# The residual add, the FP4 rewrite and retention's two decay products move off the vector engine: a two-layer macaron block on one Trainium2 core

## The reference, cut to what matters

```
def fp4_quant_dequant(x):                       # blocks of 16 along the last axis
    scale = max(max|xb| / 6, 1e-12)
    return GRID[searchsorted(MID, |xb/scale|)] * sign(xb/scale) * scale
def fp4_linear(x, w): return fp4_quant_dequant(x) @ fp4_quant_dequant(w).T
def _L1_ffn_ref(x, w_gate, w_up, w_down):
    h = silu(fp4_linear(x, w_gate)) * fp4_linear(x, w_up)      # 352 wide
    return fp4_linear(h, w_down)
def _L1_attn_ref(x, ...):                       # retention, 16 heads of 8
    scores = (Q @ K^T) * Dm / sqrt(8)           # Dm: gamma_h ** (l - m), causal
    out = scores @ V; group norm over (8 features, all tokens); @ Wout
x = x + 0.5 * _L1_ffn_ref(_layernorm(x), ...)
x = x + _L1_attn_ref(_layernorm(x), ...)
x = x + 0.5 * _L1_ffn_ref(_layernorm(x), ...)
```

## Time and profile before

| | |
|---|---|
| median of 3 runs | 1813.59 us (1809.85 to 1815.0) |
| the profiled execution, its own time | 1820.12 us |
| its span, first to last instruction | 1818.2 us |
| busy share of the span | PE 91%, DVE 77%, ACT 54%, POOL 19% |
| FP4 layer, n = 3 | about 1399 to 1535 us of the span |
| retention | about 1528 to 1688 us |
| FP4 layer, n = 5 | about 1688 to 1818 us |

### The profile page before, as it was taken

How to read it: one execution, slowest core, us unless ns; L and a number is a source line. 1 busy time by engine, 2 the same in 40 slices (tenths; PEclk the granted TensorE clock), 3 DMA queues, 4 the chain that set the end, 5 groups by cost and what they waited for, 6 DMA issues and landing times.

```text
span 1818.2 us, 30155 instructions
## 1 busy us (share of the span) xinstructions
PE 1652.5 (91%) x10801; PEld 962.2 (53%) x10801; DVE 1406.3 (77%) x2337; ACT 990.2 (54%) x1958; POOL 345.9 (19%) x661
## 2 busy tenths in 40 slices
PE   6899999879999999999999889999998788998686
PEld 5788888721111111111111248788887566665575
DVE  5765555688999999999999247655577897999895
ACT  3223333337888888888888752322333455654452
POOL 5311002461000001000000221011001135244211
PEclk9899999988999999999999979999999888999888
DMA  3000000121010100011101001000000000000000
GB/s 129 1 1 0 0 0 18 53 87 37 27 32 28 37 22 22 22 37 29 32 27 24 7 7 53 1 0 0 0 1 1 1 1 1 2 2 2 1 24 24
DMA packets 25301, 35.91 MB, mean 20 GB/s; under 512 B 5808, under 2 KB 19696, under 8 KB 24672
## 3 DMA queue, kind: packets, MB, share of 16 engines
q1 hardware_dynamic: 25184, 34.38, 6.3%
HBM read 22.57 MB, written 8.78 MB: 17 GB/s over the span
## 4 chain that ended last, share of the span: by engine, by line
PE 75%; DVE 12%; ACT 5%; issue 4%; POOL 3%; DMA 0%; SPq 0%; ACTq 0%; POOLq 0%; DVEq 0%
PE PS L968 14%; PE PS L437 12%; PE PS L956 10%; PE PS L426 7%; PE PS L427 6%; PE PS L428 6%; PE PS L945 5%; DVE neg_half L1103 3%; ACT probs L1040 3%; PE PS L1551 3%; PE PS L1633 2%; PE PS L1566 2%; POOL qk_all L1475 2%; PE PS L1643 1%; DVE qk_all L1324 1%
## 5 line engine op out<-in xcount | busy, mean ns | idle before, releaser
L1103 DVE TENSOR_REDUCE neg_half<-PS 128x2 f32<-128x1024 f32 x512 | 601.5, 1220 | 39.7 <-PE PS L945 24.8
L1040 ACT ACTIVATE probs<-PS 128x512 f32<-128x512 f32 x1024 | 529.0, 603 | 118.7 <-PE PS L956 118.4
L520 ACT ACTIVATE shared<-PS 128x512 f32<-128x512 f32 x256 | 152.7, 597 | 376.8 <-PE PS L428 364.0
L956 PE MATMUL PS<-qk_all 51*128 51x512 bf16 x1024 | 282.0, 391 | 16.9 <-ACT probs L1040 11.8
L614 DVE TENSOR_TENSOR shared<-shared,PS 128x512 f32<-128x512 f32 x256 | 174.2, 686 | 158.1 <-ACT shared L520 156.2
L968 PE MATMUL PS<-probs,Vg 128*32 128x512 f32 x2048 | 279.1, 618 | 0.0
L437 PEld LDWEIGHTS PS<-wd,shared 128*128 128x128 f32 x2048 | 250.8, 194 | 11.2 <-issue 0.5
L956 PEld LDWEIGHTS PS<-qk_all 51*128 51x128 bf16 x1024 | 71.6, 93 | 340.8 <-ACT probs L1040 321.3
L437 PE MATMUL PS<-wd,shared 128*128 128x128 f32 x2048 | 252.0, 277 | 0.0
L945 PE MATMUL PS<-qk_all 48*128 48x512 bf16 x1024 | 194.4, 392 | 17.2 <-DVE neg_half L1103 15.0
L622 DVE SCALAR_TENSOR_TENSOR x<-PS,gates,x 128x128 f32 (+1 forms) x512 | 144.1, 344 | 73.2 <-PE PS L437 73.2
(11 more groups left out here) (210 smaller groups left out, 2108.9 us busy)
## 6 DMA issues: line engine op xcount, KB each, us to landing
split<-qk_all SPq DMA_DIRECT2D x16, 384.0 KB, 3.3
qk_all<-split SPq DMA_DIRECT2D x64, 96.0 KB
qk_all<-split SPq DMA_DIRECT2D x64, 64.0 KB
qk_all<-split SPq DMA_DIRECT2D x64, 32.0 KB
shared<-OTs SPq DMA_DIRECT2D x60, 32.0 KB
probs<-in_ret_const SPq DMA_DIRECT2D x1, 1538.5 KB, 6.8
qk_all<-negT SPq DMA_DIRECT2D x96, 4.0 KB, 1.7
SC<-inverse SPq DMA_DIRECT2D x3, 512.0 KB, 5.0
```

The lines of the kernel that those rows point to most:

```text
L520: act.activation(sg[:, f, :], bank(f), ACT.Silu).then_inc(s["silu"], 1)
L956: pe.matmul(bank(RING_AT + use % RING), qs[rows, slot, 1, pair, kt * P:(kt + 1) * P], qs[rows, slot, 0, pair, half * GW:(half + 1) * GW], ...
L1040: act.activation(probs[:, n % 2, STRIPS * strip + pair, :], bank(RING_AT + use % RING), ACT.Exp, scale=ATT_SCALE).then_inc(s["exped"], 1)
L1103: dve.tensor_reduce(neg_half[m % 2][:, i % 2, :, at], bank(use_bank(i, m), 2).rearrange("p (s w) -> p s w", s=STRIPS), AX.X, ALU.max, nega ...
```

## The change

In the FP4 layers: the add to `x` is taken from DVE; instead PE multiplies the identity by each tile of `x` into bank 7 ahead of the down products, and ACT copies bank 7 to `x` (`added`), ahead of `tokensT`. POOL's scale product is split into two halves of 704 columns, each with its own signal, and PE turns the first half's tokens of two chunks while the second is still being written. ACT takes both silus of g + 1 behind the anchor of g. In retention: POOL zeroes `vm` once and then copies only the 128 values into their places; POOL makes `qd` and `kd` too, two chunks ahead; `group_rstd` moves from c = 2 to c = 3 on POOL.

```
 ffn_dve
-            def add(g):
-                dve.wait_ge(s["y"], c0 + g + 1)
-                dve.tensor_tensor(xs, bank(7), xs, ALU.add).then_inc(s["added"], 1)
...
-                if g > 0:
-                    add(g - 1)
 ffn_pool
-                pool.tensor_tensor(q_blocks(hq), q_blocks(hcode), q_wide(fscale, GT * NB_I), ALU.mult).then_inc(s["hq"], 1)
+                nb = GT * NB_I // 2
+                for k in range(PAIRS):
+                    half = slice(k * PW, (k + 1) * PW)
+                    pool.tensor_tensor(q_blocks(hq[:, half]), q_blocks(hcode[:, half]), q_wide(fscale[:, k * nb:(k + 1) * nb], nb),
+                                       ALU.mult).then_inc(s["hq"], 1)
 ffn_act
+            def added(g):
+                act.wait_ge(s["y"], c0 + g + 1)
+                xs = x[:, g * GT:(g + 1) * GT, :].rearrange("p t c -> p (t c)")
+                act.activation(xs, bank(7), ACT.Copy).then_inc(s["added"], 1)
...
-                if g + 1 < GROUPS:
-                    silu(g + 1, 0)
                 ffn_hidden_anchor(act, n, g)
                 if g + 1 < GROUPS:
-                    silu(g + 1, 1)
+                    for k in range(PAIRS):
+                        silu(g + 1, k)
                 if g + 3 < GROUPS:
                     ffn_normalise(act, n, g + 3)
+                if g > 0:
+                    added(g - 1)
                 if g + 2 < GROUPS:
                     tokensT(g + 2)
             next(lead, None)
             for c in range(len(CHUNKS)):
                 hiddenT(GROUPS - 1, c)
+            added(GROUPS - 1)
 ffn_pe
+                pe.wait_ge(s["hq"], PAIRS * (c0 + r) + 1)
+                pe.wait_ge(s["xT"], c0 + min(r + 3, GROUPS))
+                wait(pe, s["hT"], 3 * (c0 + r))
+                turned(0, 0)
+                wait(pe, s["added"], c0 + r)
+                turned(1, 0)
+                pe.wait_ge(s["hq"], PAIRS * (c0 + r + 1))
+                turned(0, 1).then_inc(s["hT_ps"], 1)
+                turned(1, 1).then_inc(s["hT_ps"], 1)
+                pe.wait_ge(s["hT"], 3 * (c0 + r) + 1)
+                turned(2, 0)
+                turned(2, 1).then_inc(s["hT_ps"], 1)
...
             def down(r):
                 pe.wait_ge(s["hT"], 3 * (c0 + r + 1))
                 for j in range(GT):
+                    pe.matmul(bank(7)[:, j * P:(j + 1) * P], ident[:, :], x[:, r * GT + j, :], start=True, stop=False)
 ret_pool
+            def masks(k):
+                pool.wait_ge(s["pj"], k + 1)
+                wait(pool, s["o_ps"], k - 2)
+                o = pj[:, k % 3, :]
+                pool.tensor_tensor(qd[:, k % 3, :], o[:, 0:P], k_qd, ALU.mult)
+                pool.tensor_tensor(kd[:, k % 3, :], o[:, 2 * P:3 * P], k_kd, ALU.mult).then_inc(s["masked"], 1)
...
+                if k == 0:
+                    pool.memset(vm[:, :, :, :].rearrange("p u j w -> p (u j w)"), 0.0).then_inc(s["vm_zero"], 1)
+                    pool.wait_ge(s["vm_zero"], 1)
                 pool.wait_ge(s["pj"], k + 1)
                 wait(pool, s["o_ps"], k - 1)
-                pool.tensor_tensor(vm[:, k % 2, :, :], vs[:, k % 3, :].unsqueeze(1).to_broadcast([P, JH, C]), k_col,
-                                   ALU.mult).then_inc(s["vm"], 1)
+                pool.tensor_copy(vm_heads[k % 2], vs[:, k % 3, :].rearrange("p (g j d) -> p j g d", g=HG, j=JH)).then_inc(s["vm"], 1)
                 if k == 0:
+                    masks(0)
                     yield
-                if b > 0 and c == 2:
+                    masks(1)
+                if k + 2 < CHUNKS_ALL:
+                    masks(k + 2)
+                if b > 0 and c == 3:
                     group_rstd(b - 1)
 ret_dve
-                if k + 2 < CHUNKS_ALL:
-                    masks(k + 2)
```

More of the change, by code:

```diff
@@ L181, in macaron @@
         qd, kd = (carve(3 * P).rearrange("p (u w) -> p u w", u=3) for _ in range(2))
-        vm = carve(2 * JH * P).rearrange("p (u j w) -> p u j w", u=2, j=JH)
+        vm_at, vm = taken[0], carve(2 * JH * P).rearrange("p (u j w) -> p u j w", u=2, j=JH)
+        HEAD_STEP = P + C // (HG * JH)
+        vm_heads = [space[:, vm_at + u * JH * P:vm_at + u * JH * P + JH * HEAD_STEP].rearrange("p (j w) -> p j w", w=HEAD_STEP)
+                    [:, :, 0:P].rearrange("p j (g e) -> p j g e", g=HG)[:, :, :, 0:C // (HG * JH)] for u in range(2)]
         rtmp, state = carve(P), carve(P)
@@ L216, in macaron @@
                     "h_raw h_anchor h_code hq hT_ps hT y added")
-        ret = stage_sems(ctx, nc, "ret", "step xn xT_ps xT proj pj qm centred masked vm scoreT decayed state o_ps o update moments "
+        ret = stage_sems(ctx, nc, "ret", "step xn xT_ps xT proj pj qm centred masked vm_zero vm scoreT decayed state o_ps o update moments "
                     "averaged gvar grstd cn y added")
@@ L1368, in ffn_codes @@
             link(q_largest(dve, hraw, amax))
-            wait(dve, ffn["hq"], c)
+            wait(dve, ffn["hq"], PAIRS * c)
             if tokens < GROUPS:
@@ L1433, in products @@
                                       ALU.mult).then_inc(s["h"], 1)
-            def add(g):
-                dve.wait_ge(s["y"], c0 + g + 1)
-                xs = x[:, g * GT:(g + 1) * GT, :].rearrange("p t c -> p (t c)")
-                dve.tensor_tensor(xs, bank(7), xs, ALU.add).then_inc(s["added"], 1)
             if n == 3:
@@ L1459, in ffn_dve @@
                 ln_stats(dve, GROUPS - 2)
-                dve.wait_ge(s["hq"], GROUPS)
+                dve.wait_ge(s["hq"], PAIRS * GROUPS)
             next(lead, None)
-            add(GROUPS - 1)
-            dve.wait_ge(s["added"], c0 + GROUPS)
             if n == 3:
+                dve.wait_ge(s["added"], c0 + GROUPS)
                 ln_stats(dve, GROUPS - 1)
@@ L1553, in gate_up, with hiddenT, turned @@
                     last.then_inc(s["gu"], 1)
[L1555 to L1568, removed]
+            def hiddenT(r):
+                def turned(c, pair):
+                    lo, w = CHUNKS[c]
+                    for j in (2 * pair, 2 * pair + 1):
+                        last = pe.transpose(bank(6 + c % 2)[0:w, j * P:(j + 1) * P],
+                                            hq[:, j * INNER + lo:j * INNER + lo + w], ident[:, :])
+                    return last
+                pe.wait_ge(s["hq"], PAIRS * (c0 + r) + 1)
[10 more added lines that the diff above has]
+                turned(2, 1).then_inc(s["hT_ps"], 1)
             def down(r):
@@ L1572, in down @@
                 for j in range(GT):
+                    pe.matmul(bank(7)[:, j * P:(j + 1) * P], ident[:, :], x[:, r * GT + j, :], start=True, stop=False)
                     for c, (lo, w) in enumerate(CHUNKS):
                         last = pe.matmul(bank(7)[:, j * P:(j + 1) * P], hqT[0:w, c, j * P:(j + 1) * P], wdT[0:w, c, :],
-                                         start=(c == 0), stop=(c == len(CHUNKS) - 1))
+                                         start=False, stop=(c == len(CHUNKS) - 1))
                 last.then_inc(s["y"], 1)
@@ L1584, in ffn_pe @@
                 if g > 0:
-                    for c in range(len(CHUNKS)):
-                        hiddenT(g - 1, c)
+                    hiddenT(g - 1)
                 if g + 1 < GROUPS:
@@ L1594, in ffn_pe @@
             next(lead, None)
-            for c in range(len(CHUNKS)):
-                hiddenT(GROUPS - 1, c)
+            hiddenT(GROUPS - 1)
             down(GROUPS - 1)
@@ L1791, in ret_dve @@
             own.turn(0)
[L1793 to L1798, removed]
             def decay(k, g):
@@ L1857, in ret_dve @@
             dve.wait_ge(ld["ret"], 32)
-            masks(0)
             for g in range(HG):
@@ L1861, in ret_dve @@
             yield
-            masks(1)
             for k in range(CHUNKS_ALL):
```

## The result

| | before | changed |
|---|---|---|
| median of the runs | 1814.3 us (4: 1809.9 to 1816.4) | 1793.03 us (4: 1790.8 to 1794.8) |
| profiled execution: time, span, mean clock | 1820.12, 1818.2, 0.946 | 1792.46, 1790.5, 0.963 |

A forecast was written before the change was run, and what follows sets the result against it. DVE with a nearly equal PE chain bounds the FP4 layers, PE batch 0, both later batches. 18 - 1.5 + 13.2 - 2.0 - 0.8 = 26.9 us off gives 1793 profiled, median 1787, range 1779 to 1799.

The forecast's parts named there:

- FP4 layers: Layers n = 3 and n = 5: 18 us saved by silu order and add, less 1.5 us where PE's ring holds turns.
- 10.7 and 8.4: FP4 turns: 10.7 us from both silus behind the anchor, 8.4 us from taking the add off DVE.
- Ring rival: FP4 turns: PE's ring holds them if the clock doesn't recover, 9 to 12 us lost, 1798; chance 0.14.
- Hand-over: From FP4 layer to retention: `added(7)` ahead of ACT's projection waits for `down(7)`, 2.9 us late, 0.9 given back; cost 2.0.
- a rival for whole layers: FP4 layers: slow-rate identity products lengthen each ring, the clock falls, kernel slower; 1820 at turns of 15.3; chance 0.04.
- Batches 1 and 2: Retention: each batch falls to 32.3 us, saving 6.3 us in batch 1 and 4.2 us in batch 2.
- DVE and PE tie at 31.2, so both drop: Retention batch: DVE's work falls to about 31.1 us, PE's floor is 31.3, so the batch falls to that level.
- Batch 3: Retention's last batch: no masks in its last two chunks and a tail bound by DVE's chain; 2.7 us saved.
- The halves: POOL's split product in FP4 layers: 0.2 to 0.3 us off the ring, a second start costs about 0.25; zero.
- The lockout rival: Retention batches 1 to 3: DVE's new state and POOL's products exclude each other, 8.2 us lost, 1795; chance 0.09.
- Tail: End of kernel: the last `down` gets eight more records, 0.95 to 1.76 us, less 0.3 for the halves; 0.8 longer.
- The signs that I had named: Changed profile: values expected for DVE's idle and waits, FP4 turns and clock, POOL's product, and score(9) to score(17).

The follow-up runs named there:

- after_again: The changed kernel profiled once more with no edit; profiled execution 1795.9 us.
- fp4_alone: The kernel before with only the four FP4-layer edits, retention as before; ratio to before 0.9939 [0.99, 0.9977].
- ret_alone: The kernel before with only retention's edits, FP4 layers as before; ratio to before 0.997 [0.9945, 0.9995].
- rstd_c2: The changed kernel with `group_rstd` put back from chunk 3 to chunk 2 of the batch; ratio to before 0.9887 [0.9839, 0.9936].
- one_product: The changed kernel with POOL's product of the hidden codes whole again instead of in halves; profiled execution 1790.71 us.

## Why the prediction was right in sign and 6 to 9 us too generous

- **The whole.** I forecast 1793 for the profiled execution, and it took 1792.46. That is luck: 11.8 of its 27.7 us less lie ahead of the edited code. From the first product to the end 15.9 us are gained, 20.2 in after_again, where I had 26.9.
- **FP4 layers, 16.5 forecast, 15.4 and 16.3 measured.** Right, and by the mechanism: DVE's own turn, 12.8 (forecast 12.9) and 13.6 (13.7). Wrong in the working: I added 10.7 and 8.4 as if each had its own worth. Alone the first is 0.5.
- **Ring rival.** It didn't come. PE is busy for 87 of 105 us, from 79, and the clock rose to 0.91 and 0.93; which of the two brought the other no run shows.
- **Hand-over, 2.0 forecast (0.5 to 4.5), 7.4 measured, 3.5 in a second profile.** This is the largest miss. I had ACT's `added(7)` wait for `down(7)`, and overlooked that `added(6)` stands ahead of the *first* part of the lead, where before ACT had gone into it while `down(6)` still ran. The size of the wait that I did see was wrong too: from 1532.03 to 1535.8 are 3.8 us, not 2.9, and the copy's 0.6 comes on top. Measured from the eighth product, score(1) comes 18.4 us behind it, 14.9 in after_again and 10.3 before: 8.1 or 4.6 late. Of that 0.7 or 1.2 is made good by score(9), about the 0.9 that I gave back, but not for my reason: fp4_alone, with DVE's products still there, makes good the same 1.2, and ret_alone nothing. With both parts of the lead ahead of the adds 41.2 is left. The further 4 us are a clock of 0.71 and 0.86 in two turns, which I had only as a rival for whole layers.
- **Batches 1 and 2, 32.3 forecast, 34.1 measured.** Batch 1's share of 6.3 started from a 38.6 that held some 2 us of slow clock. The step that failed is "DVE and PE tie at 31.2, so both drop": a sum per batch, though each chunk goes by the later of the two. Gaps of score in the changed kernel from score(9): 3.71, 4.70, 3.71, 5.53, 4.61, 4.16, 4.16, 3.49. PE's floor is 3.72, or 4.16 with Wout's records; 4.70 is 1.0 over it, 5.53 and 4.61 are 1.37 and 0.45. Together with the floor of 31.3 that is 34.1. `group_rstd` at 1.0 was right (1.1 taken out by rstd_c2); the bn_stats are shown for 0.3 of the 1.0.
- **Batch 3, 2.7 forecast, 1.0 measured**: it has the same three chunks over PE's floor.
- **POOL.** 0.455 and 0.468 us a product (0.455 forecast), memset 0.951, copy 0.296. The halves, put at zero, are worth nothing to 4 us (one_product). The lockout rival is refuted: L1852's mean was 355 ns over 24, L1870's is 345. The Trainium skill ("SBUF — State Buffer", "Who interferes with whom") says that a DVE instruction with two SBUF inputs contends with a GpSimd instruction that reads SBUF, and that the one that comes first blocks the other. The trace agrees: before, seven of DVE's 64 decay products took 0.76 to 1.36 us in place of 0.28, each beside an L1773 that had started 0.1 to 0.7 us ahead of it. In the changed kernel the two still meet, once in each of batches 1 to 3, but DVE comes first. In batch 1 L1870 starts at 1573.91 and keeps its 0.34 us, and POOL's L1786 at 1574.00 takes 0.56 us in place of 0.46.
- **Tail, 0.8 longer forecast**: 15.0 and 15.9 measured against 15.0. The 15.9 was at clock 0.66, as before's 15.0 at 0.65, so at one clock the forecast holds; the changed kernel's 15.0 was at 0.72.
- **Baseline.** I took 6.5 us between profile and median as fixed. What lies ahead of the first product alone moves by 16 us between two profiles of one kernel.
- **The signs that I had named.** DVE's idle ahead of the rounding is 6.6 us (near 6), the turns 12.8 (12.9 to 13.1), the clock 0.93 (above 0.9), POOL's product 0.455; DVE's wait for L1779 is 1.51 us (some 2), and score(9) to score(17) is 34.1 where I named 32.5.

## What to carry to other kernels

An instruction moved to another engine waits there too: list what stands behind it in that stream at the first and last turn, not only in the steady one. Two edits on a ring whose engines take turns at ending last have no separate worth; ask of each where DVE waits next if only that one is made. Where two engines tie in the sum, compare them chunk by chunk: here three chunks over PE's floor made 34.1 us of a sum of 31.3.

## What the runs showed of the hardware that was not expected

- One kernel's profiles put the same instruction 16.0 us apart, with 50 us windows at a granted clock of 0.76 or 1.00 and stretches behind it equal to 0.1 us.
- The clock of the same two turns came out at 0.71 and 0.86 or at 1.00 and 0.98, and the hand-over at 48.4 or 44.5, in three profiles of the same kernel; nothing between was seen.
- The same retention code took 5.62, 7.22 or 8.76 us from score(10) to score(11), at a granted clock of 1.00, 0.76 and 0.61.
- GpSimd's product of 128x128, 0.455 and 0.468 us, lies within 0.02 us of the line between its 32 and 512 columns (0.246 and 1.289). It takes 0.56 us where it meets a DVE instruction with two SBUF inputs that started ahead of it.
